# A four-layer graph network on one core: layer two's edge pass writes finished rows over defaults, its node pass goes, and layer three's edges run backwards

## The chip, the cores and the metric

One Trainium2 chip, one of its cores. The metric is device time in microseconds (us) from the kernel's start to its end; a lower number is better. The profile is of one execution and tells the time by engine: TensorE (PE, its weight loads PEld), VectorE (DVE), ScalarE (ACT), GpSimd (POOL), and SyncE (SP), which only issues transfers.

## What is computed

A graph of N = 50,000 nodes with rows of D = 256 fp32 values, and E = 25,000 edges, sorted by destination. Four layers, each `x = layernorm(x + layer(x))`. Layers 0 and 1 are unchanged by this case. The two that matter, cut short:

```python
# layer 2 (8 heads of 32); a node without an in-edge gets 0
ft = feat @ W;  a1 = (ft * attn_l).sum(-1);  a2 = (ft * attn_r).sum(-1)
e = leaky_relu(a1[src] + a2[dst], 0.2)
alpha = softmax of e over the edges of each dst
out = elu(segment_sum(ft[src] * alpha, dst))
# layer 3 (4 heads of 64); every node also has a loop to itself
h = x @ W.T;  a_s, a_d likewise
e = leaky_relu(a_s[src] + a_d[dst], 0.2)      # E edges and N self loops
alpha = softmax of e over each dst
out = elu(segment_sum(alpha * h[src], dst) + bias) + x
```

## The kernel before, in words

The kernel is written without a scheduler: each engine's instructions stand in the order of the code, and engines meet through counting semaphores. It is cut into stages. `barrier()` (line 234: a memset into `tick` on POOL) ends each stage on all engines, so nothing of a stage begins before the one ahead is over, its transfers too. The stages and their start times in the profile:

- stages 1 to 3 (0 to 3232 us): layers 0 and 1. Stage 3 (from 1183 us) works on the nodes in 98 steps of 512 nodes (128 partitions x J = 4), ends with `lnB`, the layer norm that gives `x2`, stores `x2` to `x2_d`, and scatters from POOL each node's row to the first of its edges (`xd_d`, line 917).
- layer 2's **edge pass**, `edge_pass(2, ...)`. The edges lie in 128 partitions, each with 196 consecutive ones, and are worked on in CS = 49 beats of J = 4 edges a partition. In a beat POOL gathers the 4 source rows (line 1181) and SP loads the 4 destination rows; PE transposes them (1226) and multiplies them with the weights and attention columns (1235, 1237), ACT evacuates the transposes (1269). VectorE then runs the `chain`: attention sums, a scan that holds the destination's value, the running maximum (lines 1337 to 1365); ACT takes `Exp` (1274); VectorE scans the sum (1320), weights the rows (1370) and adds them up along the edges, one edge after the other (1387, 1391), and divides (`divided`, 1402). POOL scatters the row at each edge that ends a destination to `tab` (1192), a table that is filled with blanks beforehand. A **tail** mends destinations that straddle two partitions: it reads back the row in `tab` (1209) and writes the mended one (1212).
- layer 2's **node pass**, `node_pass(...)`: all nodes in 98 steps; reads `x2_d` and `tab`, does the ELU (ACT 1566, 1568; DVE 1643), the residual (1650), the layer norm (bn_stats 1654, bn_aggr 1660, ACT 1576), stores `x3_d`, and, for layer 3, transposes and multiplies every node's row by layer 3's weights into `h3_d` (1544, 1555, 1583, 1629).
- layer 3's **edge pass**, `edge_pass(3, ...)`: gathers the ready products from `h3_d`; there is no matmul in its beats. Its rows go to `tab` as well, over those that layer 2 left for the same destinations.
- **last pass**, `last_pass(...)`: all nodes in 98 steps; reads `x3_d`, `h3_d` and `tab`, computes the self loop's share (small operations over pairs of steps, 1851 to 1872), scales both rows on POOL (1819, twice a step), adds them by PE into PSUM (1761), then ELU (ACT 1778, 1780; DVE 1882), residual (1886), norm (1890, 1894, POOL 1828, 1831, ACT 1787), and stores `out`.

Buffers in `arena` are used in turn (`NG` = 4 of them for the edges' rows), and each wait names the count that a buffer's last reader has reached.

Of the kernel before, what the change touches and what calls it, by code (L numbers as in the profile page):

```python
# [74 lines left out]
def wait(eng, sem, value):  # L75

    if not isinstance(value, int) or value > 0:
        eng.wait_ge(sem, value)


def gnn_program(nc, x, src, dst, ea256, ea64,
                w1_0, b1_0, gamma_0, beta_0, w2_0, b2_0, eps_0,
                u_1, w1_1, b1_1, w2_1, b2_1,
                w_2, al_2, ar_2, w_3, as_3, ad_3, bias_3, out, stop_after=9):
# [38 lines left out]
    xd_d = nc.dram_tensor("xd_d", [EP, D], F32).ap()  # L123
    fe_d = nc.dram_tensor("fe_d", [P * NS * J, 1], I32).ap()
# [3 lines left out]
    HW = D + 2 * H3  # L128
    h3_d = nc.dram_tensor("h3_d", [N, HW], F32).ap()
    ad_d = nc.dram_tensor("ad_d", [EP, H3], F32).ap()  # L130
# [13 lines left out]
    with ctx:  # L144
# [20 lines left out]
        Wg = {2: sb("Wg2", [P, FH, D + 2 * H2]), 3: sb("Wg3", [P, FH, D + 2 * H3])}  # L165
# [6 lines left out]
        bias3 = sb("bias3", [P, HW])  # L172
# [8 lines left out]
        IDX = sb("IDX", [P, 3, C], I32)  # L181
# [5 lines left out]
        CT = sb("CT", [P, P])  # L187
        fixg = sb("fixg", [P, 1], I32)
        fixs = sb("fixs", [P, 1], I32)
# [31 lines left out]
        s_c = {k: sem(f"s_c_{k}") for k in ("id", "w", "wg3", "blank", "misc", "prep", "fill0", "fe", "first", "xdz")}  # L221
# [59 lines left out]
        dF = take([C])  # L281
        dnF = take([C])
        sS = take([C], I32)
        lastF = take([C])
        dpI = take([1], I32)[:, 0:1]
        firF = take([C])
# [18 lines left out]
        def p1_sync(sp):  # L305
# [11 lines left out]
            sp.dma_start(ad_d.rearrange("(p c) h -> p (c h)", p=P), zero[:, 0:C * H3]).then_inc(s_c["xdz"], 16)  # L317

        def p1_act_loads():
# [11 lines left out]
                     (bias3[:, 0:D], bias_3.rearrange("(a d) -> a d", a=1).to_broadcast([P, D])),  # L331
# [26 lines left out]
        def p1_scalar(act):  # L358
# [33 lines left out]
            for f in range(FH):  # L392
                act.wait_ge(q["wt"], f + 1)
                act.activation(Wg[3][:, f, 0:D], psum[:, 4 + f, 0:D], ACT.Copy).then_inc(s_c["wg3"], 1)
# [4 lines left out]
        def p1_gpsimd(pool):  # L399
# [13 lines left out]
                               pattern=[[-1, P]], channel_multiplier=1).then_inc(s_c["id"], 1)  # L413
            pool.affine_select(out=lower, in_=lower, compare_op=ALU.is_gt, fill=0.0, base=0,
# [41 lines left out]
        def p1_vector(v):  # L456
# [50 lines left out]
            link(v.tensor_copy(dF, dI))  # L507
# [10 lines left out]
            link(v.scalar_tensor_tensor(out=firF, in0=dF, scalar=float(N), in1=firF, op0=ALU.is_lt, op1=ALU.mult))  # L518
# [330 lines left out]
        def p3_sync(sp):  # L849
# [17 lines left out]
            def body(k):  # L867
# [9 lines left out]
                if not (k.known() and k.s < 4):  # L877
                    store(k.plus(-4))
                if k.known() and 12 <= k.s < 12 + LATE:
                    late(k.s - 12)  # L880
# [1083 lines left out]
```

## Time and profile before

| what | us |
|---|---|
| median of 3 runs (lowest, highest) | 5746.14 (5734.33, 5750.26) |
| the profiled execution: its span | 5581.5 |
| busy in it: PE, DVE, POOL, ACT | 4162.6, 3702.1, 3611.4, 1962.3 |

The span is from the first to the last instruction that the profiler saw; the 164.6 us between it and the median lie around the program (start, end and what the device adds). Busy shares over the whole (75% PE, 66% DVE, 65% POOL, 35% ACT) are means over stages with different limits, so they are read stage by stage.

### The profile page before, as it was taken

What the parts mean: (1) busy time and instruction counts of PE and PEld (TensorE: products, weight loads), DVE (VectorE), ACT (ScalarE), POOL (GpSimd) and SP (SyncE); (2) the same over time, 40 slices, a digit from 0 to 9 for tenths busy, and PEclk for the clock granted to TensorE, in tenths of its full rate; (3) what the DMA queues carried; (4) which work ended last, traced back from release to release, by engine and by line L of the source; (5) the groups of instructions that cost most, each with busy time, mean ns of one, the idle gap of its engine ahead of it and who ended that gap; (6) DMA issues with size and microseconds to landing.
All of it is one profiled execution on the core that took longest, in us unless ns stands there. A gap on an engine that the chain in (4) does not pass through costs nothing. (4 is left out here: it accounts for less than half of the span.)

```text
span 5581.5 us, 69994 instructions
## 1 busy us (share of the span) xinstructions
PE 4162.6 (75%) x16758; PEld 2810.8 (50%) x16758; DVE 3702.1 (66%) x10203; ACT 1962.3 (35%) x3345; POOL 3611.4 (65%) x3319
## 2 busy tenths in 40 slices
PE   2276679999999999999999977776877500036666
PEld 1154445556666666666666667665666400012222
DVE  2155456666666666666666667777999665568887
ACT  0011135532222222222222222226888400026666
POOL 7488654443555556555555567775888777768887
PEclk7689889999999999999999988887999855569988
DMA  9988789985433333333333244447999733359998
GB/s 376 294 153 156 148 263 366 364 329 186 149 124 120 119 127 123 120 117 124 122 117 116 84 133 138 138 136 255 351 348 351 248 95 94 95 181 343 357 344 289
DMA packets 497175, 1129.62 MB, mean 202 GB/s; under 512 B 164007, under 2 KB 246907, under 8 KB 497031
## 3 DMA queue, kind: packets, MB, share of 16 engines
q1 hardware_dynamic: 331530, 866.20, 44.4%
q0 software_dynamic: 113184, 174.84, 12.9%
q10 hardware_dynamic: 52316, 87.06, 4.5%
q8 instruction: 41, 0.67, 0.0%
q14 instruction: 104, 0.84, 0.0%
HBM read 627.40 MB, written 543.83 MB: 210 GB/s over the span
## 5 line engine op out<-in xcount | busy, mean ns | idle before, releaser
L1067 PE MATMUL psum<-W2b,arena 128*128 128x256 f32 x3136 | 725.4, 380 | 0.0
L799 DVE TENSOR_SCALAR arena<-arena 128x256 f32<-128x256 f32 x784 | 462.6, 651 | 366.3 <-POOL arena L794 361.8
L1048 PE MATMUL psum<-arena,W1b 128*128 128x512 f32 x1568 | 699.2, 599 | 0.0
L1067 PEld LDWEIGHTS psum<-W2b,arena 128*128 128x128 f32 x3136 | 574.6, 191 | 65.2 <-issue 0.5
L1761 PE MATMUL psum<-arena,ident 128*128 128x512 f32 x784 | 409.9, 672 | 208.1 <-POOL arena L1819 206.0
L959 ACT ACTIVATE arena<-psum,hbias 128x512 f32<-128x512 f32 x392 | 269.4, 687 | 821.2 <-PE psum L1048 821.2
L1048 PEld LDWEIGHTS psum<-arena,W1b 128*128 128x128 f32 x1568 | 290.6, 190 | 401.7 <-issue 401.7
L1192 POOL DMA_INDIRECT tab<-arena,IDX x392 | 405.1, 1033 | 122.8 <-issue 91.5
L790 POOL TENSOR_TENSOR arena<-arena,lneps 128x4 f32<-128x4 f32 x196 | 41.5, 212 | 670.1 <-DVE arena L786 669.1
L1610 POOL DMA_INDIRECT ad_d<-arena,FE x392 | 394.6, 1007 | 114.3 <-issue 113.7
L917 POOL DMA_INDIRECT xd_d<-arena,FE x360 | 378.1, 1050 | 99.8 <-issue 96.9
L440 POOL DMA_INDIRECT tab<-arena x196 | 310.6, 1585 | 165.7 <-DMA tab<-zero 65.3
L1251 PE MATMUL psum<-ident,arena 128*128 128x128 f32 x24 | 5.8, 434 | 528.0 <-DVE arena L1419 516.8
L1555 PE MATMUL psum<-Wg,arena 128*128 128x264 f32 x1568 | 382.6, 400 | 19.2 <-DVE arena L1629 19.2
L1761 PEld LDWEIGHTS psum<-arena,ident 128*128 128x128 f32 x784 | 159.3, 213 | 458.0 <-issue 404.5
L1819 POOL TENSOR_TENSOR arena<-arena 128x1024 f32<-128x1024 f32 x196 | 368.3, 1900 | 10.4 <-DVE arena L1872 7.7
L1024 PE MATMUL psum<-W2a,arena 128*128 128x256 f32 x1568 | 356.9, 381 | 9.3 <-ACT arena L945 9.3
L752 PE MATMUL psum<-arena,W1a 128*128 128x512 f32 x784 | 353.7, 595 | 0.0
L702 POOL DMA_INDIRECT fe_d<-EID,FIRST x196 | 198.9, 1015 | 235.5 <-ACT arena L727 198.5
L1024 PEld LDWEIGHTS psum<-W2a,arena 128*128 128x128 f32 x1568 | 300.3, 192 | 91.6 <-issue 54.2
L1555 PEld LDWEIGHTS psum<-Wg,arena 128*128 128x128 f32 x1568 | 301.5, 197 | 76.2 <-DVE arena L1629 26.3
L577 PE MATMUL psum<-arena,NEG 128*128 128x324 f32 x500 | 161.2, 484 | 232.8 <-ACT arena L388 200.3
(256 smaller groups left out, 9286.1 us busy)
## 6 DMA issues: line engine op xcount, KB each, us to landing
arena<-tab SPq DMA_DIRECT2D x194, 544.0 KB
arena<-x_d SPq DMA_DIRECT2D x202, 512.0 KB, 7.0
arena<-in_x SPq DMA_DIRECT2D x194, 512.0 KB, 4.8
x_d<-arena SPq DMA_DIRECT2D x194, 512.0 KB, 2.9
tab<-zero SPq DMA_DIRECT2D x11, 5832.0 KB, 54.9
tab<-blank SPq DMA_DIRECT2D x97, 544.0 KB
h_d<-arena SPq DMA_DIRECT2D x97, 528.0 KB, 6.0
arena<-h_d SPq DMA_DIRECT2D x97, 528.0 KB, 5.5
```

The source lines that it names most:

```text
L440: pool.indirect_dma_start(out=tab0[:, :], out_offset=bass.IndirectOffsetOnAxis(ap=sidx[:, s, j:j + 1], axis=0), in_=comb[:, s % NC, j, :], ...
L752: last = pe.matmul(psum[:, 4 + 2 * b + g, :], W1a[:, f, g * P:(g + 1) * P], hT[:, b, f, :], start=(f == 0), stop=(f == FH - 1))
L799: v.tensor_scalar(y[:, j, :], r[:, j, :], self.mv[:, j, 0:1], self.rs[:, j:j + 1], ALU.subtract, ALU.mult).then_inc(self.s["y"], 1)
L917: pool.indirect_dma_start(out=xd_d[:, :], out_offset=bass.IndirectOffsetOnAxis(ap=FE[:, s * J + j:s * J + j + 1], axis=0), in_=x2[:, s % 2 ...
L1024: last = pe.matmul(outA(j), p3y[:, f, j * P:(j + 1) * P], W2a[:, f, :], start=(f == 0), stop=(f == FH - 1))
L1048: last = pe.matmul(psum[:, HB[c], :], W1b[:, f, c * P:(c + 1) * P], x1T[:, f, :], start=False, stop=(f == FH - 1))
L1067: last = pe.matmul(outB(j), hid[:, c, j * P:(j + 1) * P], W2b[:, c, :], start=(c == 0), stop=(c == KH - 1))
L1192: pool.indirect_dma_start(out=tab[:, :], out_offset=bass.IndirectOffsetOnAxis(ap=IDX[:, 2, c:c + 1], axis=0), in_=fin[:, s % NG, j, :], in ...
L1555: last = pe.matmul(psum[:, 2 + j, 0:HW], xT[:, k.slot(2), f, j * P:(j + 1) * P], Wg[3][:, f, :], start=(f == 0), stop=(f == FH - 1))
L1610: pool.indirect_dma_start(out=ad_d[:, :], out_offset=bass.IndirectOffsetOnAxis(ap=FE[:, c:c + 1], axis=0), in_=hs[:, k.slot(NB), j, D + H3 ...
L1761: last = pe.matmul(psum[:, b + i, :], ident[:, :], a[:, k.slot(2), 2 * i:2 * i + 2, :].rearrange("p j d -> p (j d)"), start=(n == 0), stop ...
L1819: pool.tensor_tensor(out=a[:, b, :, :].rearrange("p j (h c) -> p j h c", h=H), in0=t[:, k.slot(NB), :, 0:D].rearrange("p j (h c) -> p j h ...
```

## The change

- Stage 3 also computes layer 3's input for nodes **without** an in-edge ("lonely"). For such a node layer 2 is the norm of 2 times nothing but itself, so `x3 = x2 * lonec` with one factor a node: three small VectorE operations, one power on POOL and four activations of 256 columns on ACT a step, and a store of 512 nodes to `x3_d` on SP. All nodes get this default.
- The edge pass of layer 2 now finishes its rows: `settle` (ELU, residual and statistics, one beat late) on VectorE, `relu_exp` and `normed` on ACT, `rstd` on POOL, and scatters them over the defaults in `x3_d`. It carries the destination's row `xd2` along the edges (line 1578) in the place of `divided`, and stores each beat's raw and finished rows for later (`raw_d`, `xl_d`). Its tail also does the ELU and the norm of the mended row, with a second scatter. In its head 26 small operations in a chain build layer 3's tables.
- The node pass is dropped.
- The edge pass of layer 3 has no `h3_d` to gather from. It gathers rows of `x3_d`, loads `xl_d`, and transposes and multiplies as layer 2's does. It goes from the last edge to the first, so that a run of equal destinations begins where its row is finished. It adds the self loop's term, and scatters the row with its bias, and the self loop's share, into `tab`, whose blanks are now the bias and a share of 1.
- The last pass reads `x3_d` and `tab` alone, computes `h = x3 @ W` itself (8 transposes and 8 matmuls a step), weights it by the share (line 2114), adds the table's row and the residual **on POOL** (2082, 2087), and does the ELU's join (`unit`, 2121) on VectorE.

The core of the diff (the two edge passes are written out anew; of them the parts that the prediction speaks of):

```diff
@@ stage 3, POOL, each step
+                if s > 0:
+                    lone_pow(at(s - 1))
                 if LATE < s < NS - 1:
                     to_edges(s - 1)
...
+            lone_pow(at(NS - 1))
             to_edges(NS - 1)
@@ stage 3, ACT, each step
+                for j in range(J):
+                    act.activation(x3d[:, k.b, j, :], x2[:, k.b, j, :], ACT.Identity, bias=zero[:, 0:1], scale=lonec[:, k.b, j:j + 1]).then_inc(lonely["lrow"], 1)
@@ layer 2's edges, VectorE
-                        v.tensor_scalar(inv, sums[:, :, cur], 1e-30, None, ALU.max).then_inc(r["inv"], 1)
-                        if L == 2 and j > 0:
-                            divided(s, j - 1)
+            def settle(s):
+                c, b = s % NG, s % 2
+                wait(v, e2["ex"], s + 1)
+                wait(v, e2["S"], J * (s + 1))
+                wait(v, e2["y"], J * (s - 1))
+                v.scalar_tensor_tensor(out=rr2[:, b, :, :], in0=un2, scalar=-1.0, in1=row2[:, c, :, 0:D], op0=ALU.add, op1=ALU.max).then_inc(e2["u"].sem, 1)
...
+                v.tensor_tensor(out=rr2[:, b, :, :], in0=xd2[:, c, :, :], in1=rr2[:, b, :, :], op=ALU.add).then_inc(e2["r"].sem, 1)
...
+                    v.bn_stats(st2[:, j, :], rr2[:, b, j, :]).then_inc(e2["st"].sem, 1)
...
+                    v.bn_aggr(mv2[:, j, :], st2[:, j, :]).then_inc(e2["mv"].sem, 1)
...
+            for s in range(CS):
+                chain(s)
+                if s > 0:
+                    settle(s - 1)
+                sums_rows(s)
@@ stages
-        PHASES.append(edge_pass(2, x2_d, H2))
-        PHASES.append(node_pass(x2_d, x3_d))
-        PHASES.append(edge_pass(3, h3_d, H3))
-        PHASES.append(last_pass(x3_d, out, H3))
@@ layer 3's edges, ACT and VectorE
+            for s in range(CS):
+                ex(s)
+                if s + 1 < CS:
+                    for i in range(J):
+                        ev(s + 1, i)
+                tail(s)
@@ last pass, POOL and VectorE
+            def total(k):
+                b = k.slot(2)
+                wait(pool, lp["pr"], k.s + 1)
+                wait(pool, lp["u"], k.s - 1)
+                pool.tensor_tensor(out=l_sum[:, b, :, :], in0=l_pr[:, b, :, :], in1=l_tt[:, k.slot(NTT), :, 0:D], op=ALU.add).then_inc(lp["t"].sem, 1)
...
+                pool.tensor_tensor(out=l_ex[:, b, :, :], in0=l_ex[:, b, :, :], in1=l_xt[:, k.slot(NXT), :, :], op=ALU.add).then_inc(lp["r"].sem, 1)
...
+                v.scalar_tensor_tensor(out=l_ex[:, k.slot(4), :, :], in0=l_ex[:, k.slot(4), :, :], scalar=-1.0, in1=l_sum[:, k.slot(2), :, :],
+                                       op0=ALU.add, op1=ALU.max).then_inc(lp["u"].sem, 1)
+        PHASES.append((e2_sync, e2_scalar, e2_gpsimd, e2_vector, e2_tensor))
+        PHASES.append((e3_sync, e3_scalar, e3_gpsimd, e3_vector, e3_tensor))
+        PHASES.append((l_sync, l_scalar, l_gpsimd, l_vector, l_tensor))
```

The order of instructions shows it at three places. First, VectorE in a beat of layer 2's edge pass, from the chain's last operation (L1365; after the change L1522) on, before:

```order
L1365 TENSOR_TENSOR arena<-arena,NEG 128x32
L1320 SCALAR_TENSOR_TENSOR arena<-arena 128x40
L1370 TENSOR_TENSOR arena<-psum,arena 128x512 x2
L1380 TENSOR_SCALAR arena<-arena 128x32
L1382 RECIPROCAL arena<-arena 128x32
```

and in the changed kernel:

```order
L1522 TENSOR_TENSOR arena<-arena,NEG 128x32
L1529 SCALAR_TENSOR_TENSOR arena<-arena 128x1024
L1532 TENSOR_TENSOR arena<-arena 128x1024
L1536 BN_STATS arena<-arena 128x6 x4
L1539 MEMSET arena 128x2
L1541 BN_AGGR arena<-arena 128x2 x4
L1544 TENSOR_SCALAR arena<-arena 128x4
L1545 TENSOR_SCALAR arena<-arena 128x4
L1195 SCALAR_TENSOR_TENSOR arena<-arena 128x40
L1555 RECIPROCAL arena<-arena 128x32
L1557 TENSOR_TENSOR arena<-arena 128x64
```

The seven lines from L1529 to L1545 are `settle` of the beat ahead; they stand between the chain and the scan of the sums (L1320, now L1195), where VectorE waited for ACT's `Exp` before.

Second, ACT in a beat of layer 3's edge pass, where L1792 is `Exp`, L1787 the four evacuations of the next beat's transposes and L1797 the copy of sums and maxima into the rows to scatter. Before there were no evacuations (L1274, L1276 `Exp`, L1281 the copy):

```order
L1274 ACTIVATE arena<-arena 128x8x4
L1276 ACTIVATE psum<-arena 128x32
L1281 ACTIVATE arena<-arena 128x2x4x4
```

```order
L1792 ACTIVATE arena<-arena 128x12x4
L1787 ACTIVATE arena<-psum 128x512 x4
L1797 ACTIVATE arena<-arena 128x3x4x4
```

All four evacuations of beat s + 1 now stand behind the `Exp` of beat s.

Third, a step of the last pass on VectorE after the change (L2114 the weighting, L2121 the ELU's join, then the statistics and two small operations that give POOL the variance and the negated mean):

```order
L2114 TENSOR_TENSOR arena<-psum,arena 128x1024
L2121 SCALAR_TENSOR_TENSOR arena<-arena 128x1024
L2128 BN_STATS arena<-arena 128x6 x4
L2130 MEMSET arena 128x2
L2132 BN_AGGR arena<-arena 128x2 x4
L2135 TENSOR_SCALAR arena<-arena 128x4
L2137 TENSOR_SCALAR arena<-arena 128x4
```

and on POOL in the same step:

```order
L2082 TENSOR_TENSOR arena<-arena 128x1024
L2087 TENSOR_TENSOR arena<-arena 128x1024
L2093 TENSOR_TENSOR arena<-arena,expo 128x4
L2095 TENSOR_TENSOR arena<-arena 128x4
```

Before, both wide VectorE operations of a step (L1882, L1886) had one operand in PSUM; now L2121 has both in `arena`, and so have both wide operations on POOL.

## Rows read from the trace of the kernel before

**Rows 1.** The page's head.

```profile
span 5581.5 us, 69994 instructions
```

**Rows 2.** By stage: us, busy PE, PEld, DVE, ACT, POOL; PEclk, DMA share, GB/s.

```profile
1183.40:3232.10 2048.70, 2028.10 (x8232) 1370.70 (x8232) 1362.45 (x3237) 582.57 (x882) 1109.25 (x982) 1.00 0.39 133
3232.10:3797.70 565.60, 425.12 (x2408) 382.87 (x2408) 407.83 (x1493) 140.01 (x297) 412.95 (x397) 0.82 0.43 134
3797.70:4434.40 636.70, 482.97 (x2352) 389.46 (x2352) 553.31 (x1470) 489.83 (x784) 487.77 (x443) 0.94 0.95 327
4434.40:4954.10 519.70, 6.74 (x28) 5.98 (x28) 300.99 (x1049) 29.68 (x150) 391.06 (x397) 0.50 0.33 102
4954.10:5581.50 627.40, 409.86 (x784) 159.26 (x784) 523.91 (x1617) 404.90 (x637) 504.32 (x491) 0.90 0.91 327
```

**Rows 3.** Timeline of layer 2's edge pass, VectorE: start, duration, idle before.

```profile
3251.72 0.18 DVE L1337 COPY arena<-psum 128x16 f32<-128x16 f32 x1 [3.21 <-PE psum L1237]
...
3755.81 0.18 DVE L1337 COPY arena<-psum 128x16 f32<-128x16 f32 x1 [2.09 <-PE psum L1237]
...
3757.41 0.19 DVE L1365 TENSOR_TENSOR arena<-arena,NEG 128x32 f32<-128x32 f32 x1
3757.93 0.24 DVE L1320 TENSOR_TENSOR_SCAN arena<-arena 128x40 f32<-128x40 f32 x1 [0.33 <-ACT arena L1274]
...
3764.33 0.25 DVE L1337 COPY arena<-psum 128x16 f32<-128x16 f32 x2
...
3772.24 0.75 DVE L1402 TENSOR_TENSOR arena<-arena 128x256 f32<-128x256 f32 x2
```

**Rows 4.** By groups, POOL in 3244 to 3755 us (47 beats): busy, mean ns, idle before.

```profile
L1181 POOL DMA_INDIRECT arena<-x_d,IDX x188 | 194.2, 1033 | 67.3 <-issue 44.8 <-ACT arena L1269 13.8 <-ACT arena L1281 4.8
```

**Rows 5.** By groups, PE in the same stretch.

```profile
L1235 PE MATMUL psum<-Wg,arena 128*128 128x264 f32 x768 | 241.0, 444 | 3.5 <-DVE arena L1370 3.5
L1226 PE MATMUL psum<-ident,arena 128*128 128x128 f32 x764 | 143.2, 318 | 105.0 <-DMA arena<-x_d,IDX 105.0
```

**Rows 6.** Timeline of PE in layer 2's edge pass, after one idle gap.

```profile
3534.93 1.12 PE L1226 MATMUL psum<-ident,arena 128*128 128x128 f32 x4 [3.92 <-DMA arena<-x_d,IDX]
...
3541.05 0.63 PE L1226 MATMUL psum<-ident,arena 128*128 128x128 f32 x4
...
3542.77 0.64 PE L1226 MATMUL psum<-ident,arena 128*128 128x128 f32 x4
```

**Rows 7.** By groups, layer 2's node pass, 3900 to 4400 us, VectorE and ACT.

```profile
L1654 DVE BATCH_NORM_STATS2 arena<-arena 128x6 f32<-128x256 f32 x328 | 115.2, 413 | 4.5
L1643 DVE SCALAR_TENSOR_TENSOR psum<-arena 128x512 f32<-128x512 f32 x162 | 105.7, 698 | 0.0
...
L1576 ACT ACTIVATE arena<-arena 128x256 f32<-128x256 f32 x327 | 169.0, 587 | 88.5 <-DVE arena L1637 88.5
L1568 ACT ACTIVATE arena<-arena 128x1024 f32<-128x1024 f32 x80 | 84.6, 1058 | 2.5
```

**Rows 8.** By groups, the last pass, 5000 to 5540 us, VectorE and POOL.

```profile
L1882 DVE SCALAR_TENSOR_TENSOR psum<-arena,psum 128x1024 f32<-128x1024 f32 x88 | 107.8, 1225 | 11.0 <-ACT arena L1780 6.0 <-issue 5.0
...
L1828 POOL TENSOR_TENSOR arena<-arena,expo 128x4 f32<-128x4 f32 x88 | 89.6, 1018 | 6.9
```

**Rows 9.** By groups, stage 3, 1300 to 3100 us, POOL.

```profile
L891 POOL TENSOR_TENSOR arena<-arena,b2a 128x1024 f32<-128x1024 f32 x87 | 204.4, 2349 | 0.0
```

**Rows 10.** Timeline of stage 3: POOL's wide additions and VectorE beside them.

```profile
1187.14 2.35 POOL L891 TENSOR_TENSOR arena<-arena,b2a 128x1024 f32<-128x1024 f32 x1 [3.70 <-DMA arena<-in_x]
1187.52 1.99 DVE L977 TENSOR_SCALAR arena<-arena 128x4 f32<-128x4 f32 x1 [3.55 <-DMA arena<-tab]
...
1207.65 0.16 DVE L977 TENSOR_SCALAR arena<-arena 128x4 f32<-128x4 f32 x1
...
1208.06 2.65 DVE L982 TENSOR_TENSOR arena<-arena 128x512 f32<-128x512 f32 x1
1210.12 2.81 POOL L891 TENSOR_TENSOR arena<-arena,b2a 128x1024 f32<-128x1024 f32 x1
```

More of the change, by code:

```diff
@@ L878, in body @@
                     store(k.plus(-4))
+                if not (k.known() and k.s < 5):
+                    store3(k.plus(-5))
                 if k.known() and 12 <= k.s < 12 + LATE:
@@ L970, in body @@
                     y(k.plus(3))
-            run_steps(act, NS, body, tail=3)
+                if not (k.known() and k.s == 0):
+                    lone_rows(k.plus(-1))
+            run_steps(act, NS, body, peel=4, tail=3)
+            lone_rows(at(NS - 1))
         def p3_vector(v):
@@ L1091, in gnn_program @@
         PHASES.append((p3_sync, p3_scalar, p3_gpsimd, p3_vector, p3_tensor))
-        once = {k: sem(f"g_{k}") for k in ("zero", "end", "old", "spread", "top", "z2", "wx", "f0", "wT", "new", "fr", "row", "fix", "near")}
-        edge2 = {k: sem(f"g_{k}") for k in
-                 ("tr", "ev", "mm", "chain", "eL", "M", "d", "w", "s", "tail", "A", "B", "S", "head", "inv", "full")}
         NG = 4
-        gs = [sem(f"g_g{b}") for b in range(NG)]
-        sc = [sem(f"g_s{b}") for b in range(NG)]
@@ new lines, in gnn_program @@
+        zb2 = take([H2, P])
+        wT2 = take([H2, P])
+        mx2 = take([H2])
+        df2 = take([2, H2])
+        wf2 = take([2, H2])
+        sn2 = take([H2])
+        pick = take([P])
+        same0 = take([C])
+        few = take([6])
+        e2 = {k: Signal(sem(f"e2_{k}")) for k in
+              ("tab", "rowd", "zero", "head", "hrow", "ev", "chain", "eL", "M", "d", "w", "s", "tail", "cf", "B", "A", "S", "xc",
+               "mn", "ex", "u", "r", "nm", "end", "spread", "top", "wx", "wT", "old", "z", "wf", "new", "fix", "fixed")}
@@ new lines, in e3_sync @@
+        def e3_sync(sp):
+            slots = xl_d.rearrange("(p c j) d -> c p j d", p=P, j=J)
+            for s in range(CS):
+                wait(sp, e3["tr"], J * (s - NG + 1))
+                if s == 0:
+                    sp.dma_start(xd3[:, 0, 0:J - 1, :], slots[CS - 1, :, 0:J - 1, :]).then_inc(e3_gd[0].sem, 16)
+                else:
+                    sp.dma_start(xd3[:, s % NG, :, :], slots[CS - 1 - s, :, :, :]).then_inc(e3_gd[s % NG].sem, 16)
+            for s in range(NXT):
+                l_rows(sp, beat(s, NXT))
@@ new lines, in gnn_program, with l_rows, l_sync, tables @@
+        l_w = [e2_xl[b].after(16 * turns(b)) for b in range(NG)]
+        def l_rows(sp, k):
+            b = k.slot(NXT)
+            wait(sp, lp["r"], k.s - NXT + 1)
+            a, n = node_view(x3_d, k)
+            sp.dma_start(l_xt[0:n, b, :, :], a).then_inc(l_x[b].sem, 16)
+        def l_sync(sp):
+            def tables(k):
+                b = k.slot(NTT)
+                wait(sp, lp["t"], k.s - NTT + 1)
+                a, n = node_view(tab, k)
+                sp.dma_start(l_tt[0:n, b, :, :], a).then_inc(l_t[b].sem, 16)
+            for s in range(NTT):
+                tables(beat(s, PER))
+            def body(k):
+                if live(k.plus(NTT), NS):
+                    tables(k.plus(NTT))
+                if not (k.known() and k.s == 0) and live(k.plus(NXT - 1), NS):
+                    l_rows(sp, k.plus(NXT - 1))
+            run_beats(sp, NS, body, PER, tail=NXT)
+            for b in range(4):
+                wait(sp, l_w[b], 16 * ((NS + 3 - b) // 4))
```

1680 lines of the change are left out of this document (914 added, 766 removed).

## The prediction, made before the changed kernel had run

> **What bounds the kernel now.** I read the split by stage first, since the change leaves stages 1 and 2 alone, adds a little to stage 3, and rewrites the rest [rows 2]. Stage 3 takes 2048.7 us with PE busy for 2028.1 of them at clock 1.00: PE sets it, and ACT (582.6) and POOL (1109.3) have room. Layer 2's edge pass takes 565.6 us; no engine is busy for more than 425, the DMA engines 0.43. Layer 2's node pass takes 636.7 us at a DMA share of 0.95: transfers set it. Layer 3's edge pass takes 519.7 us with PE idle, and POOL issuing transfers. The last pass takes 627.4 us, DMA share 0.91.
>
> Then the timeline and the groups of layer 2's edge pass. POOL issues 8 indirect transfers a beat; 188 gathers, four a beat, fill the 511 us of that stretch, so a beat is 10.87 us, with little idle time at POOL that is not its own issue [rows 4]. VectorE is behind it: from the first copy of one beat (3755.81) to that of the next (3764.33) it takes 8.52 us when its input is there, 0.33 of it waiting for `Exp` [rows 3]. PE idles 105.0 us before its transposes and then runs slower: its matmuls of 264 columns take 444 ns in the mean, and transposes 318 [rows 5]. After an idle gap of 3.92 us two rows (transposes and matmuls of one J) take 6.12 us (3534.93 to 3541.05), at full speed the next takes 1.72 [rows 6]. That is the 1.2 GHz level giving way to 2.4, and it costs 6.12 - 2 x 1.72 = 2.7 us a gap here.
>
> **The change, part by part**, against the profiled execution's span of 5581.5 us [rows 1]. The 164.6 us around it are taken as unchanged, so the sum of the differences goes straight onto the median.
>
> *Stage 3: +1.4 us.* ACT gets four activations of 256 columns a step, 98 x 4 x 0.52 to 0.59 (587 ns is one of that size [rows 7]), about 205 to 230 us on top of 583 in 2049. POOL gets one power of 1.02 [rows 8] on 11.3 a step, in steps of 20.9. All are behind a PE that never waits [rows 2], and what they release is needed a step later. Should the cover fail, 98 steps at 1.3 us would be 127, but POOL is only 54% busy. At the end alone the last power (1.02 and 0.3 between) stands in POOL's queue ahead of the last scatters, and nothing covers it. The added store is 51 MB in 2049 us at a DMA share of 0.39.
>
> *Layer 2's edges: +153.* VectorE's beat is worked out from its 8.52, rounded up to 8.6 for the mean. Off: the wait for `Exp` (0.33, `settle` stands in it), and the maximum with 1e-30 (0.21). `divided` goes and the carried row comes, each four operations of 256 columns: even. On: the coefficients (0.12 and 0.22) and 0.1 for a third small one; then `settle`. Its two wide operations have both operands in SBUF; half as wide a one takes 698 ns [rows 7], and a full one with PSUM 1225 [rows 8], so 1.25 each; four bn_stats at 413 less their overlap 1.44, aggregation 0.4, two small ones 0.25: 4.6. Last, `settle` waits for `relu_exp` of the beat ahead: two activations of 1058 ns [rows 7] start when the rows end, and the chain that covers them is 1.79 us long (3755.81 to 3757.60): 0.45 with two hand-overs. Sum 13.6. POOL's beat is 10.87 and a power, a product and their gaps (1.7): 12.6, just behind. ACT (4 x 0.6, 2.1, 2.3 and small ones) is at 7.2. The beat is VectorE's, 13.6: the bound passes from POOL to VectorE. The first copy comes 19.7 us after the stage begins (3232.0 to 3251.7), the first beat has no `settle` (9.1), and the tail from the last row operation (3773.0) to the stage's end was 24.6. The 26 table operations (about 5 us) lie in the 19.7. The new tail holds `settle` (4.6), `rstd` (1.3) and `normed` (2.1) ahead of the steps that mend, then an ELU and norm of one row: 37. That is 19.7 + 9.1 + 48 x 13.6 + 37 = 718.6 against 565.6.
>
> *Node pass: -636.7* [rows 2]. Nothing of it stays.
>
> *Layer 3's edges: +124.* Three rates compete. POOL has the same 8 transfers, 10.87 at most. VectorE has layer 2's 8.5 without four divisions (1.4), the maximum and the wait (0.5), plus the addition of the bias (1.25), eight small ones in the chain (0.65) and four or five behind it (1.0): 9.6. The third is a loop: `Exp` of beat s (0.28) stands on ACT ahead of the evacuations of s + 1; the first takes 0.65 with its hand-over; then PE still has four matmul rows and three transposes, 4 x 1.72 - 0.46 = 6.4; then the chain (1.79 + 0.65 = 2.4) leads to the next `Exp`. Sum 9.8 at full clock. But in it PE idles for about 3 us of each turn (chain, `Exp`, evacuation), and that is where the trace shows the low level: the excess of [rows 5] over full speed, (444 - 387) x 768 and (318 - 273) x 764 ns, is 78 us over some 37 gaps, 2.1 us each without the small matmuls, and 2.7 in [rows 6]. I take 2.5: 12.35 a beat. So 19.7 + 49 x 12.35 + 19 (the tail; four heads, fewer than the 24.6) = 643.9 against 519.7.
>
> The Trainium skill, in "TensorE: Matmul & The Clock Gate", section "HAM oscillation — how this bites in real kernels", says that recurring idle gaps of the matmul engine keep throwing it back to the lower clock. By that rule this loop pays the restart in each beat, as forecast; without it the rate would be POOL's (the third case below).
>
> *Last pass: +125.* DMA no longer sets it: three transfers of 0.51 to 0.54 MB a step, 98 steps, are 154 MB, 471 us at the 327 GB/s of [rows 2]. POOL does two wide additions a step with both operands in SBUF, the kind that takes 2.35 us in stage 3 [rows 9], and a power, a product and gaps (1.5): 6.2. VectorE has the weighting (1.225, one operand in PSUM [rows 8]), `unit` (1.25), and statistics (2.1): 4.6. Were they independent, 6.2 would be the step. But stage 3 shows what happens when a VectorE operation on SBUF meets such an addition: a small one takes 1.99 while L891 runs (0.16 beside none), one of 512 columns takes 2.65, and the L891 that follows 2.81 in place of 2.35 [rows 10]. They exclude each other, whole operation by whole operation. Here `unit` (1.25) excludes the additions. The two small operations that end the statistics are held until the second addition ends, and behind them in VectorE's order stands the weighting (1.225), for which POOL's next addition waits. So a step is 2 x 2.35 + 1.25 + 1.225 + 0.3 for hand-overs = 7.45, with the power under the weighting. With the start (9.5) and the last steps and store (20.3) that is 97 x 7.45 + 29.8 = 752.5 against 627.4.
>
> The Trainium skill states this rule in "SBUF — State Buffer", section "SBUF: two separate sides": VectorE with two SBUF inputs and GpSimd reading SBUF hold a shared pair of ports as an exclusive lock for a whole instruction. By it the step is the 7.45 of the rows, without it 6.2, and the trace agrees.
>
> **Sum:** 1.4 + 153 - 636.7 + 124.2 + 125.1 = -233; 5746.1 - 233 = **5513 us**.
>
> **The rivals.**
>
> - *The last pass escapes the exclusion.* If the small operations fall into POOL's power, the weighting runs beside an addition, and the step is POOL's 6.2: 97 x 1.25 = 121 less, 5392. For it: the power leaves 1.5 us free in each step. Against: VectorE comes to them with no wait of its own that would move them there. 0.22.
> - *Layer 3's edges run at POOL's rate.* If PE's gaps stay short of a fall (only some of layer 2's gaps are followed by one), the beat is 10.87: 49 x 1.48 = 73 less, 5440. 0.13. Both together: 5319, 0.05.
> - *POOL's transfers wait for VectorE.* If each wide operation of `settle` holds POOL up in issuing, its beat is 12.6 + 2.5 = 15.1, 49 x 1.5 = 74 more: 5587. Against it: the gathers take 1033 ns beside a VectorE at work 72% of the time, mostly on 256-column operations in SBUF [rows 2, 4]. 0.08. The Trainium skill warns of it in "SBUF — State Buffer", section "SBUF: two separate sides": a wide-port VectorE operation keeps GpSimd from writing descriptors. The rows show no sign.
> - *Slower than before: PE at 1.2 GHz through both edge passes.* Its rows would take 3.44. Layer 3's loop is then 0.28 + 0.65 + 4 x 3.44 - 0.92 + 2.4 = 16.2, 3.8 a beat more, 188; layer 2's beat is 4 x 3.44 = 13.8 and some 1.5 of waiting, 83 more: 5784. It decides from 233 on, that is if both passes pay nearly all of it. For it: clock 0.82 in layer 2's edges [rows 2]. Against: three rows of four there run at full speed once PE is fed, and the new layer 2 feeds it with slack. 0.03.
>
> **How the numbers follow.** The forecast, 0.48, has its own range of 5465 to 5560: layer 2's beat from 13.0 to 14.2 (30 us either way), the restart from 2.1 to 2.9 (20), tails (10). The rivals hold 0.22, 0.13, 0.05, 0.08 and 0.03; 0.01 is left for others. The range goes from 5300 to 5620 and leaves out the slower case and its surroundings; below it a last pass at 6.2 with two cheap edge passes. About 0.3% (17 us) is what a measurement can tell from no change. All cases but one are faster by more than twice 0.3%: faster 0.95, the same 0.02 (the slower case half paid), slower 0.03.
>
> **What would show it.** In the profile after: layer 2's edges 700 to 740 us and VectorE without idle time in them, its seven lines of `settle` 4.6 us a beat; if POOL's indirect transfers are longer than 1.1 us, the fourth rival. Layer 3's edges 620 to 660 us with a clock under 0.9, and ACT's evacuation waiting for `Exp`; 550 to 570 at a clock of 1.00, the third. The last pass 740 to 765 us with L2135 or L2137 at over 1 us, where their kind takes 0.16; about 630 if they stay short. Stage 3 within 5 us of 2049. What would make it wrong: a beat of layer 2 in which some wait that I count as covered (`y` for the scatters, `cf` for ACT) stands open, which would show as idle time of VectorE.

## The result, and the profile after

| | median us (lowest, highest) | profiled span |
|---|---|---|
| before | 5746.5 (5734.3, 5750.3) | 5581.5 |
| changed | 6220.7 (6219.2, 6225.0) | 6217.4 |

The changed kernel is slower, by a ratio of 1.0825 (95% interval 1.0809 to 1.084). The prediction was 5513, faster. By stage, in the view by windows (us, then busy time of PE, PEld, DVE, ACT, POOL, the granted clock, DMA share, GB/s) of the changed kernel:

```profile
1185.60:4028.10 2842.50, 2291.58 (x8232) 1528.90 (x8232) 1380.59 (x3531) 741.84 (x1274) 1222.73 (x1081) 0.88 0.33 114
4028.10:4761.80 733.70, 482.76 (x2410) 419.15 (x2410) 642.55 (x2212) 326.64 (x593) 490.39 (x499) 0.78 0.51 171
4761.80:5528.30 766.50, 479.47 (x2388) 421.91 (x2388) 436.74 (x1942) 128.39 (x297) 391.31 (x396) 0.73 0.32 101
5528.30:6217.40 689.10, 506.97 (x2352) 423.14 (x2352) 520.09 (x1274) 506.02 (x784) 651.00 (x394) 0.90 0.67 222
```

Set against [rows 2], the span's 635.9 us come from here:

| stage | before | after | difference | forecast |
|---|---|---|---|---|
| 1 and 2 | 1183.4 | 1185.6 | +2.2 | 0 |
| 3 | 2048.7 | 2842.5 | **+793.8** | +1.4 |
| layer 2's edges | 565.6 | 733.7 | +168.1 | +153 |
| layer 2's nodes | 636.7 | 0 | -636.7 | -636.7 |
| layer 3's edges | 519.7 | 766.5 | +246.8 | +124.2 |
| last pass | 627.4 | 689.1 | +61.7 | +125.1 |

Stage 3 alone turns the sign. Its clock fell from 1.00 to 0.88, and PE's busy time grew from 2028 to 2292 for the same 8232 matmuls. The list of waits (in total, times, longest), ACT, POOL and PE from 2000 to 3800 us (62 steps):

```profile
ACT arena L1013 <- POOL arena L962: 824.3, 62, 13.5
...
POOL arena L813 <- DVE arena L809: 801.5, 124, 8.1
...
PE psum L1094 <- ACT arena L1006: 346.4, 62, 5.8
```

L1013 is `lone_rows`, L962 `lone_pow`, L1006 `relu`, whose result PE's `mmA` (L1094) needs. The timeline of one step, VectorE, POOL, ACT and PE, each for itself (start, duration, in brackets the idle time before and what ended it):

```profile
2501.92 0.15 DVE L1071 TENSOR_TENSOR arena<-arena 128x4 f32<-128x4 f32 x1
...
2503.25 2.35 POOL L936 TENSOR_TENSOR arena<-arena,b2b 128x1024 f32<-128x1024 f32 x1 [1.60 <-DVE arena L1075]
2505.56 1.46 POOL L962 TENSOR_TENSOR arena<-arena,expo 128x4 f32<-128x4 f32 x1
...
2507.14 2.07 ACT L1013 ACTIVATE arena<-arena,zero 128x256 f32<-128x256 f32 x4 [13.25 <-POOL arena L962]
2509.12 2.38 ACT L1006 ACTIVATE arena<-psum,hbias 128x512 f32<-128x512 f32 x4
...
2504.13 1.89 PE L1094 MATMUL psum<-W2a,arena 128*128 128x256 f32 x8
2511.56 3.78 PE L1094 MATMUL psum<-W2a,arena 128*128 128x256 f32 x8 [5.54 <-ACT arena L1006]
```

Read it from the bottom. `mmA` is the group of matmuls at L1094. PE stands still for 5.54 us in the middle of `mmA`, until `relu` of that step is done, and then runs the second half at the low clock, 3.78 us where the first took 1.89. `relu` had no operand missing. It stood behind `lone_rows` of the step before, and that waited 13.25 us for a power on POOL that stands behind both norms' powers and both wide additions of the **next** step. That power's own operand was ready a step earlier: L1071 and its neighbours of the step before made it, while the L1071 shown works for the next power.

### The profile page after: what moved, and what is told of

It reads as the page before. It is cut to its first block and busy times, and to the rows that moved or that the text cites. A ratio compares the mean times of both kernels' runs of the same rounds, so it can differ in the third digit from the quotient of the medians.

```text
span 6217.4 us, 70077 instructions
## 1 busy us (share of the span) xinstructions
PE 4593.4 (74%) x18336; PEld 3305.5 (53%) x18336; DVE 3533.6 (57%) x10296; ACT 2017.7 (32%) x3543; POOL 3460.9 (56%) x2980
## 3 DMA queue, kind: packets, MB, share of 16 engines
q8 instruction: 62, 1.02, 0.1%
## 5 line engine op out<-in xcount | busy, mean ns | idle before, releaser
L1094 PE MATMUL psum<-W2a,arena 128*128 128x256 f32 x1568 | 549.6, 512 | 534.9 <-ACT arena L1006 525.5
L1094 PEld LDWEIGHTS psum<-W2a,arena 128*128 128x128 f32 x1568 | 392.9, 258 | 687.7 <-ACT arena L1006 563.2
L1013 ACT ACTIVATE arena<-arena,zero 128x256 f32<-128x256 f32 x392 | 203.0, 588 | 1282.4 <-POOL arena L962 1282.4
L1044 DVE TENSOR_TENSOR arena<-psum,arena 128x512 f32<-128x512 f32 x196 | 134.3, 686 | 820.3 <-PE psum L1094 820.3
L2019 PE MATMUL psum<-Wg,arena 128*128 128x256 f32 x1568 | 421.3, 429 | 156.9 <-ACT arena L2037 156.9
L1750 PE MATMUL psum<-Wg,arena 128*128 128x260 f32 x784 | 285.8, 501 | 257.9 <-ACT arena L1787 257.9
L2019 PEld LDWEIGHTS psum<-Wg,arena 128*128 128x128 f32 x1568 | 330.2, 216 | 230.7 <-ACT arena L2037 154.8
L1364 PE MATMUL psum<-Wg,arena 128*128 128x264 f32 x784 | 279.9, 491 | 203.4 <-ACT arena L1399 181.3
L1710 POOL DMA_INDIRECT tab<-arena,IDX x196 | 196.4, 1002 | 293.6 <-DVE arena L1867 239.2
L1750 PEld LDWEIGHTS psum<-Wg,arena 128*128 128x128 f32 x784 | 179.5, 254 | 293.2 <-ACT arena L1787 270.0
L998 ACT ACTIVATE arena<-psum 128x512 f32<-128x512 f32 x196 | 117.0, 597 | 634.9 <-PE psum L1101 634.9
L936 POOL TENSOR_TENSOR arena<-arena,b2b 128x1024 f32<-128x1024 f32 x98 | 230.1, 2348 | 157.0 <-DVE arena L1075 154.0
```

The lines of the kernel that those rows point to most:

```text
L936: pool.tensor_tensor(out=x1b[:, k.b, :, :], in0=x1[:, k.b, :, :], in1=b2b[:, :].rearrange("p (a d) -> p a d", a=1).to_broadcast([P, J, D]) ...
L1013: act.activation(x3d[:, k.b, j, :], x2[:, k.b, j, :], ACT.Identity, bias=zero[:, 0:1], scale=lonec[:, k.b, j:j + 1]).then_inc(lonely["lrow ...
L1094: last = pe.matmul(outA(j), p3y[:, f, j * P:(j + 1) * P], W2a[:, f, :], start=(f == 0), stop=(f == FH - 1))
L1364: pe.matmul(o[:, 0:D + H2], xT2[:, j % 2, f, :], Wg[2][:, f, 0:D + H2], start=(f == 0), stop=(f == FH - 1))
L1750: pe.matmul(o[:, 0:D + H3], xT3[:, i % 2, f, :], Wg[3][:, f, 0:D + H3], start=(f == 0), stop=(f == FH - 1))
L2019: done = pe.matmul(psum[:, c + j // 2, (j % 2) * D:(j % 2 + 1) * D], l_xT[:, k.slot(2), f, j * P:(j + 1) * P], Wg[3][:, f, 0:D], start=(f ...
```

## The experiments

Each kernel was profiled; where a ratio is given it was also timed against the kernel before on the same chip.

### The kernel before, again

> The kernel before, unchanged, for its spans. In the changed kernel the profiled execution's time is 1.8 us over its span of 6217.4, while I took 164.6 us to lie around the span of before. Theory: the time around the span is under 5 us here too, and the profiled execution of before was a faster one than the 5746 of its runs; then the span is about 5740 and some stage is 160 us longer than in the first trace. Rival: 160 us lie around the span, which stays at 5580.

Measured: 5789.6 us, span 5787.9. The theory holds in its main part: 1.7 us lie around the span, so the first trace was of a quicker execution than those timed. The rest of it does not: the span is 206 us longer, not 160, and not in one stage. By windows, this one:

```profile
1185.90:3234.40 2048.50, 2027.82 (x8232) 1367.24 (x8232) 1362.30 (x3237) 582.88 (x882) 1111.46 (x983) 1.00 0.39 133
3234.40:3868.60 634.20, 474.18 (x2408) 413.34 (x2408) 409.35 (x1493) 137.17 (x297) 411.77 (x396) 0.78 0.38 119
3868.60:4553.90 685.30, 500.93 (x2352) 402.29 (x2352) 551.75 (x1470) 493.32 (x784) 481.07 (x442) 0.92 0.88 304
4553.90:5153.50 599.60, 6.73 (x28) 5.98 (x28) 306.00 (x1049) 29.71 (x150) 391.80 (x397) 0.50 0.28 89
```

The first three stages agree with [rows 2] to 3 us; layer 2's edges are longer by 69, its node pass by 49, layer 3's edges by 80, the last pass by 7. So the same code took 519.7 and 599.6 us in layer 3's edges, with no matmul in its beats. VectorE itself is slower there, in stretches. A piece of its chain, each operation needing the one ahead:

```profile
4713.22 0.18 DVE L1352 TENSOR_TENSOR arena<-arena 128x16 f32<-128x16 f32 x1 [2.62 <-remote]
4713.90 0.17 DVE L1354 SCALAR_TENSOR_TENSOR arena<-arena 128x16 f32<-128x16 f32 x1 [0.50 <-DVE arena L1352]
4714.60 0.20 DVE L1320 TENSOR_TENSOR_SCAN arena<-NEG,arena 128x20 f32<-128x20 f32 x1 [0.53 <-DVE arena L1354]
4715.30 0.18 DVE L1359 TENSOR_TENSOR arena<-arena 128x16 f32<-128x16 f32 x1 [0.50 <-DVE arena L1320]
```

They start 0.68 to 0.70 us apart, where the first trace has the same four 0.21 to 0.23 apart. Of the 255 starts of VectorE in this stage that follow an idle time of over 0.2 us, 149 come a multiple of 0.70 us behind the start ahead; in the first trace 1 of 98. What causes that is not shown; it comes back at e7.

The stage differences above hold for the spans, 635.9; by the medians the loss is 474. Against this second trace, which is like the timed executions, the changed kernel's span is 429.5 longer: stage 3 +794.0, layer 2's edges +99.5, its nodes -685.3, layer 3's edges +166.9, the last pass +54.7.

### e1: the power first in stage 3

```diff
             for s in range(NS):
+                if s > 0:
+                    lone_pow(at(s - 1))
                 if s + 2 < NS:
                     lnA.rstd(pool, at(s + 2))
...
-                if s > 0:
-                    lone_pow(at(s - 1))
```

> The changed kernel with one move: in stage 3 POOL computes lone_pow of the step before as the first thing of its step, ahead of the two norms' powers and the wide additions, and no longer behind them. All work is the same. Theory (order): ACT's lone_rows stand at the head of its queue until POOL comes to that power, and relu behind them holds up PE; with the power early the stage returns from 2842.5 to 2050 to 2070 us, the whole from 6221 to 5430 to 5460. Rival (load): the added 2.07 us on ACT, the power on POOL and the added store slow the stage by themselves; then it stays above 2600 us.

Measured: 5464.2 us, ratio 0.9458 (0.9442 to 0.9474); stage 3 takes 2064.1 us at clock 1.00:

```profile
1185.10:3249.20 2064.10, 2029.92 (x8232) 1368.80 (x8232) 1368.13 (x3531) 761.88 (x1274) 1211.20 (x1079) 1.00 0.47 157
```

All the work of the defaults is still done, and 778.4 of the 793.8 us are gone. It was the place of one POOL instruction of 1 us, and the rival (the load) is out. The load as such costs 15.4 us, most of it PE waiting 13.9 us in all for VectorE (0.9 before).

### e2 and e3: two evacuations ahead of `Exp` in layer 3's edges

```diff
             for s in range(CS):
+                if s + 1 < CS:
+                    ev(s + 1, 0)
+                    ev(s + 1, 1)
                 ex(s)
                 if s + 1 < CS:
-                    for i in range(J):
-                        ev(s + 1, i)
+                    ev(s + 1, 2)
+                    ev(s + 1, 3)
                 tail(s)
```

> The changed kernel with one move: in layer 3's edge pass ACT evacuates the first two transposes of beat s + 1 ahead of the Exp of beat s, the other two behind it, as layer 2's pass before did. Theory (a loop with PE idle in it, so that PE works at the low clock): two of the four matmul rows leave the loop, PE idles for less, the stage falls from 766.5 to 560 to 620 us. Rival (PE's rows or transfers set it by themselves): it stays within 20 us of 766.

Measured: 6188.2 us, the stage 732.6: 34 us less, not 147 to 207. The rival (within 20 us) misses as well. This stage also differs from execution to execution: in the six kernels that leave ACT's order and PE's work in it alone (the changed one, e1, e6, e7, e9, e10) it took 762.0 to 790.7 us, in the four with e2's order and no filler (e2, e3, e8, e11) 730.3 to 741.4. The order is part of the stage's length, not the main part.

> Both moves together (lone_pow first in stage 3; two evacuations ahead of Exp in layer 3's edges). If they are independent, as stages behind barriers should be, the gains add: 6221 less about 780 less about 170, so 5240 to 5300. If the clock granted in one stage depended on the one ahead, the sum would be missed by more than 20 us.

Measured: 5415.0 us, ratio 0.9373 (0.9357 to 0.9388), stage 3 2064.1, layer 3's edges 730.3. The stages keep what each move gave them by itself; the sum is above 5300 because e2's part is small.

### e4 and e5: PE kept busy in layer 3's edges

In the changed kernel VectorE's copy of the fourth row's attention (L1826) starts late. The timeline of a beat, PE, VectorE and ACT:

```profile
5105.27 2.10 PE L1750 MATMUL psum<-Wg,arena 128*128 128x260 f32 x4 [5.37 <-ACT arena L1787]
...
5113.53 0.51 PE L1752 MATMUL psum<-Wg,arena 128*128 128x8 f32 x4
5113.89 0.64 PE L1741 MATMUL psum<-ident,arena 128*128 128x128 f32 x4
5116.42 0.17 DVE L1826 SCALAR_TENSOR_TENSOR arena<-KEEP,psum 128x8 f32<-128x8 f32 x1 [4.93 <-remote]
...
5118.68 0.24 ACT L1792 ACTIVATE arena<-arena 128x48 f32<-128x48 f32 x1 [6.77 <-DVE arena L1861]
5118.83 1.06 ACT L1787 ACTIVATE arena<-psum 128x512 f32<-128x512 f32 x2
5119.46 0.80 PE L1750 MATMUL psum<-Wg,arena 128*128 128x260 f32 x1 [4.93 <-ACT arena L1787]
```

The last matmul of the beat ends at 5114.04 by its record, and the copy that waits for it alone starts at 5116.42, with a releaser that the profile can't name ("remote"). Over eight beats in a row the delay is 2.3 to 4.1 us, over 42 beats 2.98 in the mean. The loop itself is the one forecast: copy to `Exp` 2.26 (2.4 forecast), `Exp` to the next matmul 0.78 (0.93). From the first matmul (5105.27) to the copy it takes 11.15 in place of 8.9, of which PE's own records fill 8.77; the excess is the 2.38 of delay. The filler is one line:

```diff
                 wait(pe, e3["ev"], J * s + i - 1)
-                for n, a in enumerate((xs3[:, s % NG, i, :], xd3[:, s % NG, J - 1 - i, :])):
+                for again in range(7 if i == 1 and s > 0 else 1):
+                  for n, a in enumerate((xs3[:, s % NG, i, :], xd3[:, s % NG, J - 1 - i, :])):
```

> The kernel of e1 (lone_pow first; ACT's order in layer 3's edges as in the changed kernel), and in layer 3's edges PE does the second transposition group of each beat seven times in place of once: 24 needless transposes of 128 columns, about 2.8 us at full clock, in the time in which it waits for the evacuation that stands behind Exp. They write what the one group writes. Theory (clock): results of PE come 2.3 to 4.1 us later than its rows end because PE works at the low clock after each gap; with the gap filled the clock stays up, layer 3's edges fall from 789.5 in e1 to 580 to 640 us. Rival (something else delays PE's signals, for example its instructions' coming late, or the filler itself stands in the way): the stage stays over 740, since 24 instructions more a beat mend nothing.

Measured: 5419.8 us, the stage 749.4. PE's clock over the stage rose from 0.72 in e1 to 0.83. The stage is 40 us under e1's 789.5, but only 13 under the shortest of the six kernels named above, 762.0; the delay is still there (3.12 us in the mean of 41 beats, 3.39 in e1). The time is on the rival's side of the line. A mostly filled gap doesn't cure it; PE still waits 109.8 us for evacuations in 37 of these beats.

> As e4, with ACT's order of e2 too (two evacuations ahead of Exp). In e3 this order alone left the stage at 730.3. Theory (clock): with the filler it is set by POOL's 8 transfers, 10.9 a beat, 560 to 600 us in all. Rival: over 700, as e3.

Measured: 5452.7 us, the stage 772.2, which is 42 more than e3's and 31 more than the longest with this order. The rival is right. That the filler stands in PE's way, where PE has work sooner, is the likely reason, not a shown one.

### e7: markers behind PE's results

```diff
                 for h in range(2):
+                    if h == 1 and s + 1 < CS:
+                        wait(v, e3["mm"], J * s + 3)
+                        v.memset(mark3[:, 0:1], 0.0)
+                        wait(v, e3["tr"], J * (s + 1) + 1)
+                        v.memset(mark3[:, 1:2], 0.0)
                     wait(v, e3["mm"], J * s + 2 * h + 2)
```

> The kernel of e1 with two tiny VectorE memsets a beat in layer 3's edges, between the two attention copies of the chain: the first waits for the third matmul row of the beat, the second for the transposition group behind it, and then comes the copy that waits for the fourth row. They show when each of these results of PE is there, where the records of PE alone put the fourth row's end 2.3 to 4.1 us before VectorE goes on. Theory (PE works at half speed there though its records look fast): the three come spread out, about 1.7 and 3 us behind the record of the third row's end, 0.9 and 2.6 us apart. Rival (a stall of PE, or a late signal, at the end alone): the first two come within 0.2 us of the recorded ends and only the fourth row's result is late. The stage itself stays at 750 to 790 us, 0.15 us a beat more.

The timeline of one beat of this kernel, PE and then VectorE (L1828 and L1830 are the markers, L1832 the copy):

```profile
4254.11 0.51 PE L1753 MATMUL psum<-Wg,arena 128*128 128x8 f32 x4
4254.48 0.63 PE L1742 MATMUL psum<-ident,arena 128*128 128x128 f32 x4
...
4255.83 0.51 PE L1753 MATMUL psum<-Wg,arena 128*128 128x8 f32 x4
...
4255.83 0.06 DVE L1828 MEMSET arena<- 128x1 f32 x1 [2.16 <-PE psum L1753]
...
4257.26 0.06 DVE L1830 MEMSET arena<- 128x1 f32 x1 [1.38 <-PE psum L1742]
...
4260.10 0.17 DVE L1832 SCALAR_TENSOR_TENSOR arena<-KEEP,psum 128x8 f32<-128x8 f32 x1 [2.78 <-remote]
```

By the records the three results are ready at 4254.62, 4255.11 and 4256.34. They reach VectorE 1.2, 2.2 and 3.8 us later: 1.43 and 2.84 apart, where the records have 0.49 and 1.23. The delay grows from result to result; so it isn't one late signal at the end, and the rival as worded is out. But the theory's numbers, 0.9 and 2.6 apart, are missed too.

Over the 41 beats of 4080 to 4720 us the first interval is 0.72 to 0.75 (4 beats), 1.41 to 1.46 (34) or 2.12 to 2.13 (3), and the second 1.44, 2.1, 2.8 to 2.9 or 3.5 in all but one: multiples of 0.71. PE at 1.2 GHz has no such step; at that level a transposition group takes 0.88 and a matmul row 2.6 in this stage. The step is the one that VectorE shows in the kernel before, where PE had nothing to do (`before_again`). And ACT takes the last transposition group that it needs in the beat shown 0.04 us after its recorded end (5111.14 in the changed kernel). So a rival that no run was made for fits the steps better: an engine that has stood idle goes on late. ACT does it too where it waits in e3: it starts at 4308.41 and 4317.11, 5.1 and 4.4 us behind the recorded ends of its transposes. PE at half speed is neither shown nor excluded, and the cause of the delay stays open.

The stage took 790.5, as e1's 789.5. But the last pass, in which nothing was edited, fell from 689.2 to 607.0 us.

### e9 and e10: a buffer 8 and 16 bytes further on

The markers' tile had moved one buffer of the last pass, `l_xt`, by 8 bytes within its partition.

```diff
-        cursor[0] = max(cursor[0], e3_end)
+        cursor[0] = max(cursor[0], e3_end) + 2
         l_xt = take([NXT, J, D])
```

> The kernel of e1 with nothing changed but the place of the last pass's row buffer l_xt in a partition: 8 bytes further on. In e7 a small tile ahead of it moved it by 8 bytes, and the last pass fell from 689 to 607 us, POOL's residual addition from 2360 to 2000 ns. Theory (the operand's address): the same here, 607 us and 2000 ns. Rival (something else in e7 did it): 689 us and 2360 ns.

> As e9, with l_xt 16 bytes further on than in e1, which puts it at a multiple of 64 bytes, as the other operand l_ex is. Theory A (the two operands' offsets from each other within 16 bytes matter, e1 has them equal, e9 8 bytes apart): 2360 ns and 689 us as in e1. Theory B (alignment to 64 bytes matters): another value than e1's, 2000 ns or less.

The groups of POOL's wide additions of the last pass in e9 (busy, mean ns; L2082 adds the table's row, L2087 the residual from `l_xt`):

```profile
L2082 POOL TENSOR_TENSOR arena<-arena 128x1024 f32<-128x1024 f32 x68 | 160.4, 2358 | 0.0
L2087 POOL TENSOR_TENSOR arena<-arena 128x1024 f32<-128x1024 f32 x67 | 134.0, 2000 | 0.0
```

and in e10:

```profile
L2082 POOL TENSOR_TENSOR arena<-arena 128x1024 f32<-128x1024 f32 x59 | 144.5, 2449 | 5.3 <-DVE arena L2114 4.4 <-issue 0.9
L2087 POOL TENSOR_TENSOR arena<-arena 128x1024 f32<-128x1024 f32 x60 | 141.7, 2362 | 0.0
```

Last pass 607.5 and 689.7 us, whole kernels 5359.8 and 5436.7. The address does it, and theory A fits: with the operands' offsets equal within 16 bytes the addition takes 2.36 us, with 8 bytes between them 2.00. Alignment to 64 bytes (e10) gives nothing. One rival is left: in every quick case it is the second operand that starts 8 bytes past a multiple of 16, the first at a multiple; no run moved the first, or both.

Here 0.36 us of POOL in each of 98 steps would be 35 us; 82 were gained. The groups say where: POOL's four operations of a step take 2453, 2360, 1491 and 453 ns in e1 and 2359, 2000, 1012 and 639 in e7, 0.75 us less a step, and its idle time shrinks by 0.09; 98 x 0.84 is 82. The addition's own part is 0.36 of it; the largest is the power, which VectorE's `unit` now meets no more. VectorE's held L2135 also fell, from 1045 ns to 543 (L2141 in e7).

### e6, e8 and e11: the last pass, and all together

e6 is e1 with the residual addition on VectorE (POOL's goes), behind `unit`, and the statistics ahead of it; the core of the edit:

```diff
                 weighted(k)
-                if not (k.known() and k.s < 1):
-                    unit(k.plus(-1))
                 if not (k.known() and k.s < 2):
                     stats(k.plus(-2))
+                if not (k.known() and k.s < 1):
+                    unit(k.plus(-1))
+                    residual(k.plus(-1))
```

> The kernel of e1, and in the last pass the residual addition goes from POOL to VectorE, which does weighting, statistics of two steps ago, join and residual in this order. POOL's step then is 2.35 + 1.5 + one lock-out of at most 1.2 = about 5; VectorE's is 3 x 1.22 + 2.2 = 5.9, and its two operations with both operands in SBUF exclude POOL's one addition only. Theory (POOL's two additions and the exclusion set the step of 6.8): 6.0 a step, the pass falls from 689 to 600 to 625 us. Rival (each wide VectorE operation on SBUF waits for POOL's addition in full): over 7.2 a step, 730 us or more.

Measured: 5402.0 us, the pass 625.2. That is the theory's value, at the upper end of its range: VectorE is busy for 584 us of it.

> The changed kernel with the three moves that helped: lone_pow first in stage 3 (e1), two evacuations ahead of Exp in layer 3's edges (e2), the residual of the last pass on VectorE (e6). The stages are behind barriers, so the gains should add: 5462 of e1, less 34 to 60 for layer 3's edges, less 64 for the last pass: 5340 to 5370, against about 5775 of the kernel before on the same chip, a ratio of 0.925 to 0.93.

Measured: 5354.0 us, ratio 0.925 (0.9231 to 0.9269), as expected.

> Stage 3's and layer 3's moves (e3), the residual left on POOL, and both of POOL's wide additions in the last pass with their operands 8 bytes apart within 16 (l_xt as in e9, and the table buffer l_tt moved against the product). Theory (the address relation is what counts): both additions take 2000 ns, the step is 2 x 2.0 + 1.2 + one lock-out of up to 1.2, 5.6 to 5.8, the pass 565 to 590 us, the whole 5300 to 5330. Rival (only l_xt's own place counts): the first addition stays at 2360 ns, the pass at 607, the whole 5335 to 5360.

```profile
L2092 POOL TENSOR_TENSOR arena<-arena 128x1024 f32<-128x1024 f32 x69 | 138.0, 1999 | 0.0
L2087 POOL TENSOR_TENSOR arena<-arena 128x1024 f32<-128x1024 f32 x69 | 137.8, 1998 | 0.0
```

Measured: 5314.9 us, ratio 0.9252 (0.922 to 0.9285); the pass 594.9, against 607.5 in e9. Both additions take 2.00 us now: theory A holds for a second pair of operands. The pass is 5 us over the expected range; POOL's product (L2100) takes longer, 824 ns where it takes 639 in e7. The ratios of e8 and e11 are the same within their intervals, as the kernel before was also quicker on e11's chip (5749.2 against 5781.6); the pass itself gained 30 us. By its median this is the fastest version of the study; by the ratio e8 and e11 are level, some 7.5% under the kernel before.

## Why the prediction was wrong

- **The step that failed** is "Stage 3: +1.4 us", in the sentence "All are behind a PE that never waits, and what they release is needed a step later". I priced the added operations by their durations against each engine's free time, and that was nearly right: e1 carries them at 15.4 us. What I left out was to name what is queued behind the instruction that waits. `lone_rows` is the last thing of ACT's step, and the power that it waits for stands in POOL's next step behind two other powers and two wide additions; behind `lone_rows` on ACT stands the next `relu`, and PE waits for that. It cost 793.8 us, 8.1 a step, of which 5.6 is PE's wait (346.4 in 62); the rest is near the 2.7 a step by which PE's busy time grew at the lower clock. The fallback that I gave, 127 us, was for a lack of capacity, not for an order.
- **"The 164.6 us around it are taken as unchanged"** failed too. Only 1.8 us lie around a span; the first trace was of a quick execution. Taken against the second trace of before, the dropped node pass alone was worth 685 and not 637, and the 164.6 us were work of the stages.
- **Layer 2's edges** were right in mechanism and size: 733.7 against 718.6. VectorE is busy for 642.6 of it, and in 640 us of beats it waits for little (19.5 us ahead of `settle`). Most of the small excess is the carried row, 477 ns an operation where I set it even with the division's 418 (four a beat, 11 us in all):

```profile
L1578 DVE SCALAR_TENSOR_TENSOR arena<-arena,KEEP 128x256 f32<-128x256 f32 x187 | 89.2, 477 | 0.0
...
L1529 DVE SCALAR_TENSOR_TENSOR arena<-arena 128x1024 f32<-128x1024 f32 x47 | 57.6, 1225 | 19.5 <-issue 13.6 <-ACT arena L1416 6.0
```

  It stayed at 733.6 to 735.7 in every kernel. The fourth rival does not set the stage, though half of its sign is there:

```profile
L1304 POOL DMA_INDIRECT x_d<-arena,IDX x177 | 199.9, 1129 | 54.4 <-issue 43.7 <-ACT arena L1423 10.7
L1298 POOL DMA_INDIRECT arena<-x_d,IDX x170 | 179.0, 1053 | 46.0 <-issue 40.5 <-PE psum L1353 2.7 <-ACT arena L1423 2.7
L1310 POOL TENSOR_TENSOR arena<-arena,expo 128x4 f32<-128x4 f32 x44 | 45.9, 1043 | 60.6 <-DVE arena L1545 60.6
```

  A gather takes 1053 ns (1033 before), a scatter 1129 (1063 before), over the 1.1 us that I had named. But that is under 0.4 us a beat, and POOL stands idle 1.4 us a beat (60.6 in 44) until VectorE's last operation of `settle`.
- **Layer 3's edges**: the loop was right, but "12.35 a beat" measured (766.5 - 38.7) / 49 = 14.9, between the forecast and the 16.2 of the slower rival. The sum also has a slip of 0.05 (9.8 + 2.5 is 12.3). By PE's records the restart of 2.5 us was sized well: rows and restart together took 8.77 in the beat shown above, 8.9 forecast. The term that failed is the hand-over from PE's fourth row to VectorE's copy, which I put at nothing. It took 0.04 us in each of 34 beats of layer 2's edges in the first trace, and 2.98 in the mean here, 122.6 us over the forecast for the stage. Whether PE ends later than its records or VectorE starts late is open (e7). The third rival (POOL's rate) is out.
- **Last pass**: the exclusion is there, the place was wrong. Of the small operations the first waits for POOL's **first** addition (L2135 1074 ns in the mean, L2137 157), slips in between the two, and the weighting then runs beside the second. The step is POOL's: 2.45 + 2.36 + 1.51 + 0.44 = 6.8, with the weighting's 1.22 hidden and only `unit` (in the power's 1.51 where it takes 1.02) left of the exclusion. 7.45 was too much by 0.65, 63 us (its own terms add to 7.475). The Trainium skill's rule ("SBUF — State Buffer", section "SBUF: two separate sides": whoever starts first holds the shared ports for a whole instruction, the other waits) agrees with L2135, and with the power, which as a GpSimd operation that reads SBUF is held by `unit`; I had applied it to the additions alone.

```profile
L2135 DVE TENSOR_SCALAR arena<-arena 128x4 f32<-128x4 f32 x81 | 87.0, 1074 | 9.9
...
L2082 POOL TENSOR_TENSOR arena<-arena 128x1024 f32<-128x1024 f32 x81 | 198.1, 2446 | 6.6 <-DVE arena L2114 5.9 <-issue 0.6
...
L2093 POOL TENSOR_TENSOR arena<-arena,expo 128x4 f32<-128x4 f32 x81 | 122.6, 1514 | 0.0
```

With stage 3 mended (e1, 5464 us) the kernel lies 0.9% under the forecast of 5513, but that is luck. Against the forecast e1's span has 1.7 us too much ahead of stage 3, 14.0 in it, 15.8 in layer 2's edges and 145.6 in layer 3's, and 63.4 too little in the last pass: 113.7 more in all. The 164.6 us counted on top of the span, of which 1.8 exist, more than make up for it.

## What to carry to other kernels

When an addition puts a producer on one in-order queue and its consumer on another, write down for both queues what stands between the operand's being ready and the instruction, and what stands behind it; the engines' free time says nothing about that. An operation that depends on the last step goes to the head of the step, where its operand is already there. Before the difference of two spans is added to a median, look whether the profiled execution is one like those timed.

## What the hardware showed that I had not expected

- POOL's addition of two 1024-column fp32 operands takes 2.36 us when both start at the same offset within 16 bytes, 2.00 when the second starts 8 bytes further on within 16 (e9, e10, and a second pair in e11). A tile of two words elsewhere made a pass 82 us faster (e7).
- POOL's power of 4 columns, 1.02 us alone, took up to 2.06 in the last pass, 2.03 of it beside VectorE's `unit` with both operands in SBUF (POOL 5824.38, VectorE 5824.32). I had counted powers as free of the exclusion.
- After a wait VectorE took PE's results 2 to 4 us later than PE's records end (e7), at intervals that are multiples of 0.71 us; in the first trace of before it took them 0.04 us after. The same step of 0.70 stands between VectorE's own operations in a stage in which PE does nothing (`before_again`). Why stays open.
- The same code's edge and node passes differed by 49 to 80 us between two executions (519.7 and 599.6 for layer 3's edges), while stages 1 to 3 agreed to 3 us. The changed layer 3's edges differed by 29 us between kernels that leave them alone.
